# Sparsemax in batch 0: halved sums on GpSimd and four tiles sorted ahead of the count

## What is computed

```
y = layernorm(x)
scores = (y Wq + bq)_h . keys_h / 4          # 16 heads, 32 patterns a head
z_sorted = sort(scores, descending); cum = cumsum(z_sorted)
k = number of j with 1 + j * z_sorted_j > cum_j
tau = (cum_k - 1) / k
A = max(scores - tau, 0)                      # sparsemax over the 32 patterns
x = x + layernorm((A values) Wo + bo)
x = x + layernorm(block2(layernorm(x)))       # dispatch attention, 16 experts, combine attention
```

## Time and profile before

| | us |
|---|---|
| median of 3 runs | 493.5 |
| lowest and highest | 493.32, 499.21 |
| the profiled execution | 498.5 |
| its span, first to last instruction | 496.4 |
| TensorE busy in the span | 399.7 |
| VectorE busy | 308.8 |
| ScalarE busy | 231.6 |
| GpSimd busy | 149.0 |

### The profile page before, as it was taken

One profiled execution on the slowest core, in us unless ns is written; L12 is line 12 of the kernel. 1 busy time (PEld: TensorE's weight loads), 2 busy tenths in 40 slices (PEclk: granted clock), 3 DMA queues, 4 the chain that ended last, 5 costly groups with the idle time before them and its releaser, 6 DMA issues.

```text
span 496.4 us, 6944 instructions
## 1 busy us (share of the span) xinstructions
PE 399.7 (81%) x2072; PEld 248.6 (50%) x2072; DVE 308.8 (62%) x1177; ACT 231.6 (47%) x422; POOL 149.0 (30%) x253
## 2 busy tenths in 40 slices
PE   3875767669799956659899989999997569999981
PEld 3532323225455532436687666744443226888871
DVE  3599999979996958352642443433332214969984
ACT  2236546747668658355857463300000001356765
POOL 3105645465765260321311030010000000335453
PEclk9998787979889977697999999999999989999997
DMA  4293011011010271317546667549999999901223
GB/s 149 79 304 121 1 43 42 1 43 44 1 42 3 74 273 77 110 42 255 212 140 239 218 220 286 191 154 383 387 401 388 396 379 374 337 3 44 85 85 127
DMA packets 44029, 83.77 MB, mean 169 GB/s; under 512 B 1878, under 2 KB 36316, under 8 KB 39388
## 3 DMA queue, kind: packets, MB, share of 16 engines
q1 hardware_dynamic: 42936, 82.15, 46.8%
q10 hardware_dynamic: 1060, 1.22, 0.8%
HBM read 70.78 MB, written 12.58 MB: 168 GB/s over the span
## 4 chain that ended last, share of the span: by engine, by line
PE 55%; DVE 19%; ACT 8%; DMA 6%; issue 6%; POOL 3%; SPq 1%; DVEq 1%; ACTq 0%; POOLq 0%
PE bank L1476 6%; PE bank L1452 6%; PE bank L1052 6%; PE bank L1119 5%; PE bank L1365 5%; PE bank L1085 5%; PE bank L1148 5%; DVE top L1615 4%; PE bank L1074 3%; DMA scr<-in_L_ffn_e_W_dram 3%; DMA work<-in_L_ffn_e_Wg_dram 2%; DVE exc L1646 2%; PE bank L1064 2%; PE bank L1111 2%; ACT d L741 2%
## 5 line engine op out<-in xcount | busy, mean ns | idle before, releaser
L1052 PE MATMUL bank<-Wz,yT 128*128 128x512 f32 x128 | 71.0, 707 | 24.0 <-DVE top L1615 22.6
L1052 PEld LDWEIGHTS bank<-Wz,yT 128*128 128x128 f32 x128 | 28.3, 230 | 60.8 <-issue 50.6
L1615 DVE MAX8 top<-bank 128x8 f32<-128x32 f32 x512 | 51.6, 186 | 4.1 <-ACT scr L734 2.4
L986 ACT ACTIVATE d<-d 128x32 f32<-128x32 f32 x16 | 3.7, 229 | 88.5 <-DVE d L1966 88.5
L1085 PE MATMUL bank<-aWo,hoT 128*128 128x256 f32 x128 | 39.3, 433 | 3.5 <-DVE arena L1734 3.5
L575 POOL TENSOR_SCALAR veps<-mv 128x4 f32<-128x4 f32 x24 | 5.7, 236 | 110.8 <-DVE mv L1543 83.6
L682 POOL TENSOR_TENSOR work<-work 128x512 f32<-128x512 f32 x16 | 16.6, 1059 | 64.6 <-DVE work L2031 64.6
L1734 DVE TENSOR_TENSOR arena<-bank,Wz 128x256 f32<-128x256 f32 x16 | 6.7, 418 | 45.2 <-PE bank L1085 45.1
L713 ACT ACTIVATE arena<-arena,shift,rstd 128x256 f32<-128x256 f32 x64 | 33.2, 596 | 2.6 <-POOL shift L697 2.6
L1074 PE MATMUL bank<-heads 128*64 128x256 f32 x128 | 22.8, 436 | 11.5 <-issue 5.8
L1085 PEld LDWEIGHTS bank<-aWo,hoT 128*128 128x128 f32 x128 | 23.6, 204 | 14.1 <-issue 10.2
(11 more groups left out here) (256 smaller groups left out, 863.4 us busy)
## 6 DMA issues: line engine op xcount, KB each, us to landing
arena<-in_L_ffn_e_W_dram SPq DMA_DIRECT2D x10, 1024.0 KB, 8.6
x<-in_L_ffn_e_W_dram SPq DMA_DIRECT2D x9, 1024.0 KB, 10.2
arena<-in_L_ffn_e_Wg_dram SPq DMA_DIRECT2D x7, 1024.0 KB, 11.1
scr<-in_L_ffn_e_W_dram SPq DMA_DIRECT2D x7, 1024.0 KB, 13.6
work<-in_L_ffn_e_W_dram SPq DMA_DIRECT2D x5, 1024.0 KB, 13.8
xin<-in_L_attn_query_dram SPq DMA_DIRECT2D x8, 512.0 KB, 4.0
x<-in_L_attn_query_dram SPq DMA_DIRECT2D x1, 4096.0 KB, 16.5
out_dram<-x SPq DMA_DIRECT2D x8, 512.0 KB, 3.3
```

Of the source, the lines that this page charges most:

```text
L1052: mm = pe.matmul(bZ[t % 2][:, :], yT[:, c, t * P:(t + 1) * P], Wz[:, c, :], start=(c == 0), stop=(c == C - 1))
L1615: mx = v.max(top[:, h * TG + t, :], bZ[t % 2][:, h * NS:(h + 1) * NS])
```

## The change

GpSimd adds, after each clamp of batch 0, the first and the second 16 values of each short row of `d` into a new place `halved` (1,024 values a partition). This stands between `subtract` and `roots`. VectorE's sum in batch 0 reads `halved`, once the add is done. VectorE sorts all four tiles of group i+1 before the count of group i. ScalarE copies tiles 2 and 3 of group i+1 right behind the clamp, ahead of `mark` and `norm_y`. Batch 1 and TensorE's order stay as they are.

```diff
+        halved = arena[:, 12288:13312]
...
+            def add_halves(i):
+
+                hold(relued, i * 2 + 2)
+                rows_ = d[:, :].rearrange("p (r s) -> p r s", s=NS)
+                pool.tensor_tensor(halved.rearrange("p (r s) -> p r s", s=NS // 2), rows_[:, :, 0:NS // 2],
+                                   rows_[:, :, NS // 2:NS], ALU.add).then_inc(added, 1)
...
             with pool.Fori(0, GB - 1) as i:
                 subtract(i, 0)
+                add_halves(i)
                 roots(0, i + 2)
                 lower(i, 0)
             subtract(GB - 1, 0)
+            add_halves(GB - 1)
             roots(0, GB + 1)
             lower(GB - 1, 0)
...
             with act.Fori(0, GB - 2) as i:
                 clamp(i)
+                put_scores(i + 1, 0, range(2, TG))
                 mark(i)
                 norm_y(i + 2)
-                put_scores(i + 1, 0, range(2, TG))
                 put_yT(i + 2)
                 put_scores(i + 2, 0, range(2))
                 signs(i, 0)
...
+                elif b == 0:
+                    hold(added, i + 1)
+                    v.tensor_reduce(exc[:, :], halved.rearrange("p (r s) -> p r s", s=NS // 2), AX_X, ALU.add).then_inc(newton, 1)
                 else:
                     v.wait_ge(relued, i * 2 + 2)
                     v.tensor_reduce(exc[:, :], d3, AX_X, ALU.add).then_inc(newton, 1)
...
             def batch_of_scores(i, b, last=False):
 
                 first_statistics(i + 2)
-                sort_top(i + 1, range(2))
+                sort_top(i + 1, range(TG))
                 count(i, b, True)
                 settle(i, b, True, last)
-                sort_top(i + 1, range(2, TG))
                 threshold(i + 1)
```

More of the change, by code:

```diff
@@ L250, in build @@
         diff = sem("diff")
+        added = sem("added")
         relued = sem("relued")
@@ L836, in _ @@
             clamp(2)
+            put_scores(3, 0, range(2, TG))
             mark(2)
             norm_y(4)
-            put_scores(3, 0, range(2, TG))
             put_yT(4)
@@ L844, in _ @@
             clamp(3)
+            put_scores(4, 1, range(2, TG))
             mark(3)
             norm_y(5)
-            put_scores(4, 1, range(2, TG))
             put_yT(5)
```

## The result

| | before | after |
|---|---|---|
| median, us (6 runs each) | 493.76 | 512.88 |
| lowest and highest | 493.32, 499.21 | 509.39, 514.81 |
| ratio, with its 95% interval | | 1.0346 [1.0296, 1.0397] |
| the profiled execution, and its span | 498.5, 496.4 | 510.04, 508.1 |
| TensorE, VectorE, ScalarE, GpSimd busy | 399.7, 308.8, 231.6, 149.0 | 399.9, 315.9, 232.3, 160.8 |

The change makes the kernel slower, by 19.1 us where 11.1 was forecast. All that the profiles show of it lies in batch 0: its check is 15.4 us later, and the rest of the span is not longer (386.5 after, 390.2 before). Executions of the kernel before lie between 492.9 and 499.2 us, and the profile shown before is of a long one, 498.5; the last experiment looks at that.

A forecast was written before the change was run, and what follows sets the result against it. Two almost equal loops bound batch 0: VectorE's own work and the round through the other engines. The round grows from 17.4 to 19.4 us, the check comes 11.1 later: 493.5 + 11.1 = 504.6, range 497.8 to 508.8.

The forecast's parts named there:

- the move: Batch 0: all four tiles of group i+1 sorted ahead of the count, so VectorE waits for the third tile's copy.
- the half-length sum: VectorE's sum in batch 0 reads 1,024 values, not 2,048: 1.22 us, saving 1.07 a group.
- The wait of `norm_y` for the root behind the add: ScalarE's `norm_y` waits for GpSimd's `roots`, queued behind the add: add 1.91 us, roots with its gap 2.03.
- a round: Batch 0, clamp end to clamp end through add, roots, `norm_y`, `turn_y`, `put_yT`, scores, copy, `signs`: 19.4 us against 17.4.
- the delay is passed on whole: After batch 0: batch 1 and the expert weights' transfers follow the check, so its 11.1 us delay reaches the end.
- `threshold` is 3.12 and stays: VectorE, from the scan's start to the end of `tau`: 3.12 us before, and unchanged after.
- VectorE's loop: VectorE's own work per group, busy 16.38 of 17.36 us before; the change was to make it shorter.
- My row of that size: Trace row for GpSimd's add: two subtractions of 1,024 values in 3.78 us, so 1.9 each; add taken as 1.91.
- TensorE's pairs in the round: Matmuls of two tiles after `turn_y`, taken at the slow clock: 5.41 us until ScalarE takes the second.
- the last step: From the last `tauf` to batch 0's check, set by `lower` (3.64) and `signs` (2.0): 6.0 us, before 6.2.
- the 509.6 of the sum: Whole kernel: the profiled execution's 498.5 us with the check's 11.1 us delay passed on whole.
- the clock alone at its worst: Upper end of the range: score pairs near fully 1.2 GHz, 6.8 us each, three times, +4.2, so 508.8.

The follow-up runs named there:

- the last experiment: Further profiled executions of both kernels, with nothing altered: the kernel before at 498.36, 494.47 and 494.0 us, the changed kernel at 511.09 and 510.57.
- the rk kernel: The changed kernel with rk, the small operand of VectorE's multiply in `threshold`, read from PSUM for groups 0 to 4: 510.97 us, ratio 1.0319.
- filled gaps alone: The changed kernel with unread TensorE products in each group of batch 0, 16 before `turn_y` and 3 before the scores after it: 516.87 us, ratio 1.0429.
- the add-only kernel: The kernel before with GpSimd's add and the half-length sum, the sorts and ScalarE's order as before: 505.83 us, ratio 1.0211.

## Why the prediction was right in its sign and too low

**Right: the move costs more than the half-length sum saves.** The sum fell to 1.20 (1.22 forecast), and VectorE waited 1.3 to 3.0 us for the third tile. The add was hidden from the count. The wait of `norm_y` for the root behind the add is real, but hardly binds here: 0.2 us in group 1, nothing in groups 0 and 3, where `mark` ended later, since the copy of the third tile before it had waited for TensorE. In groups 1 to 3 of the rk kernel, which has the same queues, it is 1.8 to 1.9. The clamps ended at 64.5, 84.7 and 105.0, where 64.1, 83.5 and 102.9 were forecast: a round of 20.2 to 20.3, not 19.4. That the delay is passed on whole held too: the rest of the span is 386.5 to 387.3 in the changed kernel and 387.2 to 387.6 in the shorter executions of the one before.

**Wrong: "`threshold` is 3.12 and stays".** It is 5.9 (53.33 to 59.25): the multiply takes 3.94 beside `lower`, and 0.69 there as soon as rk is in PSUM. I moved `lower` beside `threshold` and asked only what that does to the next subtraction, not what the two engines do to each other. The tau of groups 1 to 3 was 2.9, 3.9 and 4.5 late against the forecast. VectorE's loop, which the forecast had shorter than the round, became as long as it (20.2 from T(1) to T(2)). So the round hid most of the delay, and the rest came out at the end.

**Mis-sized.** The add measured 2.37, not 1.91. My row of that size, the subtraction, has `tau` broadcast as one operand; that this makes it the shorter is not tested. By the estimate from the Trainium skill's "GPSIMD Engine Reference", section "Elementwise — side-by-side cycle accounting", it would have been 2.2, and that was nearer than my row. TensorE's pairs in the round were slower: 5.59, 5.86 and 5.93 for 5.37, and 5.73, 5.99 and 5.96 until ScalarE took the second tile, for 5.41. `lower` at 4.42, for 3.64, stood in the last step.

The check, forecast at 117.3, started at 121.63. The 4.3 are: clamp(3) 2.1 late (`norm_y` began 0.3, 0.6 and 0.5 later behind its clamp, mainly for the add; the pairs took 0.3, 0.6 and 0.6 more; the way from the turn to the pair 0.2 to 0.5 less); the third tile's copy 1.4 behind that clamp, since tau was late and TensorE's pair began late (106.40 against 104.99); `lower` 0.8 longer. So by this sum the blocking accounts for 2.2; with rk in PSUM the median was 1.9 lower, too little to confirm it.

The forecast fell 8.0 us short of the 19.1 of the medians. Of that, 4.3 are these; 1.5 are that I summed from an execution of 498.5 and added to a median of 493.5: batch 0 of the shorter executions is 1.4 shorter, which the move takes away too. The rest of the span gives 0.5 back, and 2.8 stay open. That the profiled execution, at 510.04, is so near the 509.6 of the sum for it is luck: its check came 4.3 late, and the rest of its span was 3.7 shorter than in the execution that the sum started from.

**The range** ended at 508.8 because it priced the clock alone at its worst. It had no bound for VectorE beside GpSimd, for which the trace of the kernel before had the sign: the running sum took 1.67 where it met the end of `lower`, and 1.23 where it did not. With that I could have bounded `threshold` by the end of `lower`.

## What to carry to other kernels

Where a step is moved so that two engines work at the same time that did not before, look at what each of them reads: here a VectorE instruction with two SBUF operands waited until GpSimd's 2,048-value subtraction was done. Before relieving a loop, write down the length of the next one; here rk in PSUM alone gave 1.9 us or nothing and filled gaps alone cost 4.0, the roots first on top of rk gave 4.3 us in batch 0 and no clear change of the time, and all of them together with chain in PSUM 13. An instruction added to a queue is paid by what stands behind it: in the add-only kernel `norm_y` waited 2.6 to 2.7 us for the roots behind the add, besides the 2.3 to 4.4 that the sum waited for the add itself.

## What the runs showed of the hardware

The two instructions of `threshold` with both inputs in SBUF and GpSimd's `lower` held each other up until the one that began first was done or nearly done. In the changed kernel `lower` ran from 53.57 to 57.98 and the multiply from 54.58 to 58.52: it ended 0.54 after `lower`, where it takes 0.69 alone. `lower` itself took 0.77 more than its 3.64 while the running sum, which had begun before it, was finishing. With rk in PSUM the multiply was free, with chain in PSUM `lower` was. The Trainium skill says this in "SBUF — State Buffer", section "Who interferes with whom": a VectorE instruction with two SBUF inputs contends with a GpSimd instruction that reads SBUF. The traces agree for `lower`. The sorts (from PSUM) ran beside `lower` in the kernel before at their usual 3.23 and were not held. Nor was every two-input instruction beside every GpSimd one: in the add-only kernel the foldings of `above` ran from 65.20 to 66.34, with their usual 1.14, over GpSimd's root of 128x4 values (64.67 to 65.71).

TensorE's granted clock moved between the two levels with the order of the work, and an idle time of 2.2 to 3.0 us was followed by either: 3.67 after 2.98 in the changed kernel, 5.15 after 2.45. With two of the three gaps of a round filled, the third grew to 5.5 to 5.9 us, and the pair behind it was at 5.20 to 6.53.
